# The feed-forward half of a decoder layer as one stage: gate, then up, then down, with the gate's extremes searched per tile

## The chip, the cores and the metric

One Trainium2 chip, one of its cores. The metric is the device time of one execution in microseconds (us). The kernel before takes 3091.08 us, the median of three runs (3089.62 to 3091.11).

## What is computed

A decoder layer on x of 16 x 512 rows of 512 numbers: gated linear attention, a decaying scan with a context, and a quantised feed-forward block, each followed by a residual and a layer norm. The change concerns the feed-forward block, which is

```python
def act_qdq(x):
    scale = max(max(abs(x)) / 32767, 1e-12)
    return clip(round(x / scale), -32768, 32767) * scale
x = act_qdq(x)
up = act_qdq(x @ lpbq_dequant(w_up).T)          # 512 -> 1536
gate = act_qdq(x @ lpbq_dequant(w_gate).T)      # 512 -> 1536
sig = fixed_qdq_u16(sigmoid(gate))              # steps of 2**-16
gate = act_qdq(gate * sig)
o = act_qdq(gate * up)
return o @ lpbq_dequant(w_down).T               # 1536 -> 512
```

The scale of each `act_qdq` is the largest magnitude of a whole tensor. So `gate` can't be rounded before all its products are known, nor `o` before its own largest value is.

## The kernel before, in words

`decoder` (L1630) runs five stages, each ending in a barrier of all engines: `prepare_weights`, `attention_phase`, `up_gate_phase` (L840), `scales_phase` (L1096) and `down_phase` (L1378). The first two are not changed. There are NB = 16 steps b of 512 rows. A step has 12 tiles of `up` and 12 of `gate`, each 128 outputs by 512 rows in one bank of PSUM; four tiles make a chunk of 128 x 2048 (48 chunks of each kind). Every engine has its program written out by hand, and the order within it is that of the code; semaphores join them.

**Up and gate.** `up_gate_phase` splits each operand into a high and a low float32r part (`qh`, `ql`, `wh`, `wl`), so a tile is 4 x 3 matmuls (L1062 to L1064). TensorE takes 24 tiles a step, groups of four of up and gate in turn. ScalarE evacuates each tile into a chunk `group` (L951) and takes the silu of gate chunks (L958). VectorE takes the largest magnitude of up chunks (L1001), the largest and the smallest product of gate chunks (L1004, L1005), and of silu times up (L1008, L1011), all in chunks of 2048 from SBUF. SyncE stores every chunk (L909). The next step's input is rounded on VectorE (L988), transposed by TensorE (L1054) in two halves after tiles 11 and 13, copied by ScalarE (L941), and its low part taken by VectorE (L993).

**Scales.** `scales_phase` reduces the maxima over the partitions (L1201, after one at the start of up and gate, L924), works the scales out in tiny VectorE instructions, decides (L1299) whether two chunks suffice to find the largest |o|, and loads these two chunks again (L1175, L1176), rounds and multiplies them whole, and reduces once more (L1209). TensorE has nothing to do meanwhile.

**Down.** `down_phase` loads every chunk of gate and up again as float32. GpSimd rounds both (L1485, L1490); ScalarE takes the sigmoid and rounds twice (L1515, L1519, L1524) and makes the high part (L1531); VectorE rounds the sigmoid (L1558), multiplies twice (L1560, L1566) and makes the low part (L1570), adds the residual (L1578) and takes statistics (L1581). TensorE does 48 matmuls a chunk (L1616 to L1618) into 8 banks, four for each of two steps. VectorE's order around a chunk is set by `chunk_steps` (L1425): a chunk is begun, the one before carried on, the one before that finished.

```python
                    pe.matmul(o, wh[:, m, k], qh[:, par, k], start=(k == 0), stop=False)
                    pe.matmul(o, wh[:, m, k], ql[:, par, k], start=False, stop=False)
                    mm = pe.matmul(o, wl[:, m, k], qh[:, par, k], start=False, stop=(k == KC - 1))
```

Of the kernel before, what the change touches and what calls it, by code (L numbers as in the profile page):

```python
# [837 lines left out]


def up_gate_phase(nc, x2_dram, w_ffn_t, up_dram, gate_dram, amax_x2, acc, rmax, scales):  # L840

    NM = 2 * MT
    GM = 4
    NG = NM // GM
    with ExitStack() as ctx:
        used = []
        ctx.callback(lambda: (nc.clear_and_free_semaphores(used), nc.all_engine_barrier()))  # L849

        def sb(name, shape, dt=F32):
            return ctx.enter_context(nc.sbuf_tensor(name, shape, dt))

        def sem(name):
            return phase_semaphore(nc, used, name)

        wh = sb("ug_wh", [P, NM, KC, P], F32R)
        wl = sb("ug_wl", [P, NM, KC, P], F32R)
        w_stage = sb("ug_w_stage", [P, 2, GM, KC * P])
        x2 = sb("ug_x2", [P, TT, HID])  # L860
        qh = sb("ug_qh", [P, 2, KC, T], F32R)
        ql = sb("ug_ql", [P, 2, KC, T], F32R)
        group = sb("ug_group", [P, 4, CH])
        silu = sb("ug_silu", [P, 2, CH])
        ident = sb("ug_ident", [P, P])
        step_max = sb("ug_step_max", [P, 3, 3])
        turn_ps = [ctx.enter_context(nc.psum_tensor(f"ug_turn{i}", [P, T], F32)) for i in range(2)]
        out_ps = [ctx.enter_context(nc.psum_tensor(f"ug_out{i}", [P, T], F32)) for i in range(6)]

        w_in = [sem(f"ug_w_in{i}") for i in range(2)]  # L870
        wh_ready, wl_ready = sem("ug_wh_ready"), sem("ug_wl_ready")
        x2_in = sem("ug_x2_in")
        stored = [sem(f"ug_stored{i}") for i in range(4)]
        consts, amax_all, scale_ready, inv_ready = sem("ug_consts"), sem("ug_amax_all"), sem("ug_scale_ready"), sem("ug_inv_ready")
        tq_ready, turned, qh_ready, ql_ready = sem("ug_tq_ready"), sem("ug_turned"), sem("ug_qh_ready"), sem("ug_ql_ready")
        out_ready, evacuated, silu_ready, prod_ready, rmax_ready = (
            sem("ug_out_ready"), sem("ug_evacuated"), sem("ug_silu_ready"), sem("ug_prod_ready"), sem("ug_rmax_ready"))
        step_max_ready, acc_ready = sem("ug_step_max_ready"), sem("ug_acc_ready")
        s_x, inv_x = scales[:, 0:1], scales[:, 1:2]

        def group_of(w, g):
            return w[:, g * GM:(g + 1) * GM].rearrange("p m k n -> p m (k n)")

        def slot(par, g):
            return (NG * par + g) % 4

        with nc.Block() as block:
            @block.sync
            def _(sp):
                sp.dma_start(x2[:], x2_dram[0]).then_inc(x2_in, 16)  # L890

                def load_weights(g):
                    if g < NG:
                        group_at = NWG // 3 * (g % 2) + g // 2
                        wait(sp, wl_ready, g - 1)
                        sp.dma_start(w_stage[:, g % 2], w_ffn_t[group_at]).then_inc(w_in[g % 2], 16)
                load_weights(0)
                load_weights(1)

                def step(b, par, nxt, first=False):  # L900
                    if nxt:
                        sp.wait_ge(turned, KC * (b + 1))
                        sp.dma_start(x2[:], x2_dram[b + 1]).then_inc(x2_in, 16)
# [193 lines left out]

# [584 lines left out]
```

## Time and profile before

| | us |
|---|---|
| median of three runs | 3091.08 |
| span of the profiled execution | 3087.7 |
| its own time (span and launch) | about 3.4 more than the span, taken from the median |
| attention and weights, until the first up/gate matmul | 1294.5 |
| up and gate, TensorE | 1294.5 to 2369.8 |
| TensorE idle (scales, start of down) | 2369.8 to 2460.6 |
| down, TensorE | 2460.6 to 3076.1 |
| busy: TensorE, VectorE, ScalarE, GpSimd | 2757.5, 2280.7, 1327.2, 588.0 |

Only the second half of the table can change, so it is to be read stage by stage: which engine is busy in it, and which wait holds TensorE.

### The profile page before, as it was taken

Reading aid. Unit: us, or ns where it says so; the run is one execution under the profiler, and the core shown is the slowest. Engines: PE = TensorE matmul, PEld = TensorE weight load, DVE = VectorE, ACT = ScalarE, POOL = GpSimd, SP = SyncE. Lnnn points to the kernel's source line nnn. Section 1 sums busy time; section 2 is a strip of 40 time slices with the busy share of each in tenths; the row PEclk is TensorE's granted clock in tenths of the full one; section 3 lists DMA queues with packets and bytes.
Section 4 is the critical chain, followed back from the end, with each engine's and each line's share of the span. In section 5 each row is a group of like instructions: output and inputs, shape, how many; then the busy total and the mean of one; then the engine's idle time right before and its main releaser. Section 6 shows DMA issues by size and latency. Waiting matters only on the chain. (4 is left out here: it accounts for less than half of the span.)

```text
span 3087.7 us, 32437 instructions
## 1 busy us (share of the span) xinstructions
PE 2757.5 (89%) x12272; PEld 2261.6 (73%) x12272; DVE 2280.7 (74%) x2242; ACT 1327.2 (43%) x1396; POOL 588.0 (19%) x266
## 2 busy tenths in 40 slices
PE   2589999999999999599999999999997198988988
PEld 2477777777777777488888888888885177777776
DVE  8678988889888998565555555555555688888886
ACT  2233433444333433243333333333333466666664
POOL 4111111112111111000000000000000485555552
PEclk7789999999999999899999999999998599999999
DMA  6211111111111111332222322222223555555552
GB/s 238 96 41 62 68 54 54 68 60 69 54 54 63 66 54 42 124 140 104 109 109 109 122 109 109 109 102 104 107 109 135 207 205 216 217 217 217 216 206 82
DMA packets 58129, 357.18 MB, mean 116 GB/s; under 512 B 6496, under 2 KB 6496, under 8 KB 17248
## 3 DMA queue, kind: packets, MB, share of 16 engines
q1 hardware_dynamic: 54480, 330.33, 28.5%
q10 hardware_dynamic: 3600, 26.22, 2.1%
q8 instruction: 29, 0.48, 0.1%
q14 instruction: 20, 0.16, 0.0%
HBM read 212.87 MB, written 143.65 MB: 115 GB/s over the span
## 5 line engine op out<-in xcount | busy, mean ns | idle before, releaser
L1062 PE MATMUL ug_out<-ug_qh,ug_wh 128*128 128x512 f32 x1536 | 601.3, 391 | 2.8 <-DVE ug_ql L993 1.4
L1064 PE MATMUL ug_out<-ug_qh,ug_wl 128*128 128x512 f32 x1536 | 598.5, 390 | 0.0
L1063 PE MATMUL ug_out<-ug_ql,ug_wh 128*128 128x512 f32 x1536 | 598.1, 389 | 0.0
L951 ACT ACTIVATE ug_group<-ug_out,scales 128x512 f32<-128x512 f32 x384 | 263.2, 690 | 607.3 <-PE ug_out L1064 604.5
L1616 PE MATMUL dn_ps<-down_wh,dn_oh 128*128 128x512 f32 x768 | 314.4, 409 | 148.3 <-DVE dn_ol L1570 148.3
L1004 DVE TENSOR_REDUCE ug_step_max<-ug_group 128x1 f32<-128x2048 f32 x48 | 109.7, 2285 | 335.4 <-ACT ug_group L951 335.4
L1062 PEld LDWEIGHTS ug_out<-ug_qh,ug_wh 128*128 128x128 f32 x1536 | 288.8, 188 | 62.6 <-DVE ug_wl L1016 2.0
L1064 PEld LDWEIGHTS ug_out<-ug_qh,ug_wl 128*128 128x128 f32 x1536 | 288.6, 188 | 60.5
L1063 PEld LDWEIGHTS ug_out<-ug_ql,ug_wh 128*128 128x128 f32 x1536 | 288.9, 188 | 59.0
L1617 PE MATMUL dn_ps<-down_wl,dn_oh 128*128 128x512 f32 x768 | 310.6, 404 | 0.0
L1618 PE MATMUL dn_ps<-down_wh,dn_ol 128*128 128x512 f32 x768 | 310.2, 404 | 0.0
L1616 PEld LDWEIGHTS dn_ps<-down_wh,dn_oh 128*128 128x128 f32 x768 | 151.8, 198 | 187.3 <-DVE dn_ol L1570 155.1
L717 PE MATMUL qk_ps<-xh,wah 128*128 128x512 f32 x512 | 201.4, 393 | 26.8 <-DVE xl L531 26.8
L1198 POOL MEMSET sc_magic<- 128x1 f32 x1 | 0.1, 99 | 1094.0 <-POOLq L849 1094.0
L718 PE MATMUL qk_ps<-xl,wah 128*128 128x512 f32 x512 | 200.7, 392 | 0.0
L721 PE MATMUL qk_ps<-xh,wal 128*128 128x512 f32 x512 | 200.6, 392 | 0.0
L449 ACT ACTIVATE phi<-qk_ps 128x1024 f32<-128x1024 f32 x64 | 65.9, 1029 | 263.6 <-PE qk_ps L721 263.6
L1001 DVE TENSOR_REDUCE ug_step_max<-ug_group 128x1 f32<-128x2048 f32 x48 | 109.7, 2286 | 90.3 <-ACT ug_group L951 90.3
L1617 PEld LDWEIGHTS dn_ps<-down_wl,dn_oh 128*128 128x128 f32 x768 | 152.3, 198 | 32.2
L1618 PEld LDWEIGHTS dn_ps<-down_wh,dn_ol 128*128 128x128 f32 x768 | 151.4, 197 | 33.0
L1485 POOL TENSOR_SCALAR dn_gate<-dn_gate,scales 128x2048 f32<-128x2048 f32 x48 | 168.6, 3512 | 0.0
L1515 ACT ACTIVATE dn_gs<-dn_gate,scales 128x2048 f32<-128x2048 int16 x48 | 96.6, 2013 | 152.3 <-POOL dn_gate L1485 152.3
(211 smaller groups left out, 5712.6 us busy)
## 6 DMA issues: line engine op xcount, KB each, us to landing
up_products<-ug_group SPq DMA_DIRECT2D x48, 1024.0 KB, 3.9
gate_products<-ug_group SPq DMA_DIRECT2D x48, 1024.0 KB, 3.9
dn_gate<-gate_products SPq DMA_DIRECT2D x48, 1024.0 KB, 4.9
dn_up<-up_products SPq DMA_DIRECT2D x48, 1024.0 KB, 4.8
xt_raw<-in_xT SPq DMA_DIRECT2D x64, 256.0 KB, 2.8
csq<-in_ctx_rows SPq DMA_DIRECT2D x16, 1024.0 KB, 6.7
xrow<-in_x_rows SPq DMA_DIRECT2D x16, 1024.0 KB, 4.8
x_rows<-xrow SPq DMA_DIRECT2D x16, 1024.0 KB, 3.9
```

Of the source, the lines that this page charges most:

```text
L717: pe.matmul(out, sh, mh, start=(k == 0), stop=False)
L718: pe.matmul(out, sh, ml, start=False, stop=False)
L721: mm = pe.matmul(out, sl_, mh, start=False, stop=(k == n - 1))
L951: act.activation(group[:, n % 4, m * T:(m + 1) * T], out_ps[(g * GM + m) % 6][:], ACT.Copy, scale=s_x).then_inc(evacuated, 1)
L1001: dve.tensor_reduce(step_max[:, 0, q:q + 1], part, AX.X, ALU.max, apply_absolute_value=True).then_inc(step_max_ready, 1)
L1062: pe.matmul(o, wh[:, m, k], qh[:, par, k], start=(k == 0), stop=False)
L1063: pe.matmul(o, wh[:, m, k], ql[:, par, k], start=False, stop=False)
L1064: mm = pe.matmul(o, wl[:, m, k], qh[:, par, k], start=False, stop=(k == KC - 1))
L1485: pool.tensor_scalar(gate[:, n], gate[:, n], inv_g, MAGIC, ALU.mult, ALU.add).then_inc(g_round, 1)
L1616: pe.matmul(o, oh[:, n, k, rows], mh, start=(n == 0 and k == 0), stop=False)
L1617: pe.matmul(o, oh[:, n, k, rows], ml, start=False, stop=False)
L1618: mm = pe.matmul(o, ol[:, n, k, rows], mh, start=False, stop=(n == NC3 - 1 and k == KC - 1))
```

## The change

The three stages become one, `ffn_phase`, with three passes over the 16 steps and no barrier between them. First all gate tiles (12 a step), then all up tiles, then down.

- **Gate pass.** TensorE transposes x2 as loaded, unrounded. ScalarE rounds while it evacuates (float32 in PSUM to int16 `q16`), then makes `hi` from it; VectorE makes `lo`. SyncE stores the rounded input to DRAM. After ScalarE has evacuated a tile, VectorE takes the largest and the smallest product from the PSUM bank itself, and the bank is free only after both.
- **Between gate and up.** The gate's scale and that of gate x sigmoid are worked out before the up pass.
- **Up pass.** The rounded input comes back from DRAM. Gate chunks are loaded, made int16 and sigmoid by ScalarE, the sigmoid is made uint16 by GpSimd, and one VectorE instruction gives the rounded product `gs16`, which is stored as int16. VectorE also takes the chunk's largest |up|, the product gs16 x up, and its maximum per 512 columns.
- **Scales.** Two pieces of 512 columns, instead of two chunks, are looked at again.
- **Down pass.** It loads up (float32) and gs16 (int16). GpSimd makes `up16`, VectorE the rounded product `o16` in one instruction, ScalarE `hi`, VectorE `lo`.
- **Weights.** There is room for 12 tiles, not 24: the up and down weights are loaded and split when the tiles of the last pass that use their place are done.

The core of the diff (the old phases go out whole, as told above):

```diff
+                def turn(b, par, tiles):                       # TensorE
+                    for c in tiles:
+                        wait(pe, q_ready, KC * b + c - 1)
+                        for j in range(TT):
+                            mm = pe.transpose(turn_ps[c % 2][:, j * P:(j + 1) * P],
+                                              x2[:, par, j * HID + c * P:j * HID + (c + 1) * P], ident[:])
+                def tile(s, par, m, first, gate):
+                        pe.wait_ge(evacuated, MT * s + m - 5)
+                            pe.wait_ge(gate_max_ready, 2 * (MT * s + m - 5))
+                def step(s, par, turn_next=False, weights=None, first=False, gate=True):
+                    pe.wait_ge(lo_ready, KC * (s + 1))
+                    for m in range(MT):
+                        if weights is not None and m % GM == 0:
+                            pe.wait_ge(wl_ready, weights + m // GM + 1)
+                        tile(s, par, m, first, gate)
+                        if m == 5 and turn_next:
+                            turn(s + 1, 1 - par, (0, 1))
+                        if m == 7 and turn_next:
+                            turn(s + 1, 1 - par, (2, 3))
...
+                def quantize(b, par):                          # ScalarE
+                    for c in range(KC):
+                        act.wait_ge(turned, KC * b + c + 1)
+                        act.activation(q16[:, par, c], turn_ps[c % 2][:], ACT.Copy, scale=inv_x).then_inc(q_ready, 1)
+                        act.wait_ge(q_ready, KC * b + c + 1)
+                        act.activation(hi[:, par, c], q16[:, par, c], ACT.Copy).then_inc(hi_ready, 1)
+                def gate_step(b, par, ahead, first=False):
+                    for g in range(NG):
+                        evacuate(b, par, g, range(GM))
+                        if first and g < NG - 1:
+                            weights_high(g + 1)
+                        if g == 1 and ahead:
+                            quantize(b + 1, 1 - par)
+                def up_step(b, par, ahead, first=False):
+                    for g in range(NG):
+                            act.wait_ge(up_max_ready, NG * (b - 1) + g + 1)
+                            act.wait_ge(prod_ready, NG * (b - 1) + g + 1)
+                        evacuate(NB + b, par, g, (0, 1))
+                            gate_chunk_16(nb, npar, ng, first and ng > 0)
+                        evacuate(NB + b, par, g, (2,))
+                            gate_chunk_sigmoid(nb, npar, ng)
+                        evacuate(NB + b, par, g, (3,))
+                        if first and g < NG - 1:
+                            weights_high(NG + g + 1)
+                        if not ahead:
+                            weights_high(2 * NG + g)
+                        if g == 1 and ahead:
+                            high(b + 1, 1 - par)
...
+                def gate_step(b, par, ahead, first=False):     # VectorE
+                    for g in range(NG):
+                        if g == 2 and ahead:
+                            low(b + 1, 1 - par)
+                        if first and g > 0:
+                            weights_low(g)
+                        for m in range(GM):
+                            dve.wait_ge(evacuated, n + 1)
+                            dve.tensor_reduce(gate_max[:, 0, bass.ds(n, 1)], ps, AX.X, ALU.max).then_inc(gate_max_ready, 1)
+                            dve.tensor_reduce(gate_max[:, 1, bass.ds(n, 1)], ps, AX.X, ALU.min, negate=True).then_inc(gate_max_ready, 1)
+                def up_step(b, par, ahead, first=False):
+                    for g in range(NG):
+                        if g == 2 and ahead:
+                            low(NB + b + 1, 1 - par)
+                        if first and g > 0:
+                            weights_low(NG + g)
+                        dve.wait_ge(evacuated, GM * (NG * (NB + b) + g + 1))
+                        dve.tensor_reduce(up_max[:, bass.ds(t, 1)], group[:, g], AX.X, ALU.max, ...)
+                        dve.tensor_tensor(prod[:, 0], gs16[:, g], group[:, g], ALU.mult).then_inc(prod_ready, 1)
+                        dve.wait_ge(prod_ready, t + 1)
+                        dve.tensor_reduce(cell_max[:, bass.ds(GM * t, GM)], prod[:, 0]..., AX.X, ALU.max, ...)
+                        if g < NG - 1 or ahead:
+                            gated(nb, npar, ng)     # scalar_tensor_tensor: gs16 <- sr16 (u16), g16 (i16)
+                def down_step(b, par, k=None, bias=True, ahead=True):
+                    product(b, par, 1)              # scalar_tensor_tensor: o16 <- gs16 (i16), up16 (i16)
+                    ol_chunk(b, par, 0)
+                        norm_bias(b - 2)
+                    product(b, par, 2)
+                    ol_chunk(b, par, 1)
+                        sums(b - 1, 1 - par, k)
+                        product(b + 1, 1 - par, 0)
+                    ol_chunk(b, par, 2)
...
+                def round_sigmoid(b, par, g, first=False):     # GpSimd, up pass
+                    pool.tensor_scalar(sr16[:, (NG * par + g) % 2], raw[:, g], 65536.0, 0.0, ALU.mult, ALU.add)
+                def round_up(b, par, g, first=False):          # GpSimd, down pass
+                    pool.tensor_scalar(up16[:, (NG * par + g) % 2], raw[:, g], inv_u, 0.0, ALU.mult, ALU.add)
...
+                def down_loads(b, par, k, ahead):              # SyncE
+                        sp.wait_ge(d_stored[par], 16 * k)
+                    sp.dma_start(x2_res[:, par], x2_dram[b]).then_inc(d_x2_in[par], 16)
+                        for g in range(NG):
+                            sp.wait_ge(up16_ready, t + 1)
+                            sp.dma_start(raw[:, g], up_dram[t + NG]).then_inc(d_up_in[g], 16)
+                            sp.wait_ge(o16_ready, t + 1)
+                            load_gs(b + 1, g)
```

## Rows read from the trace of the kernel before

**Rows 1.** Stages by --windows: busy time of each engine, then granted clock, DMA share, GB/s.

```profile
1380.00:2344.00 964.00, 964.00 (x4366) 800.47 (x4365) 535.40 (x299) 346.36 (x444) 0.00 (x0) 1.00 0.27 108
...
2470.00:3055.00 585.00, 527.39 (x2181) 429.10 (x2180) 511.59 (x389) 400.61 (x238) 336.03 (x147) 0.94 0.56 204
```

**Rows 2.** TensorE's timeline where stages meet: start, duration, then what it waited for.

```profile
1294.47 0.79 PE L1062 MATMUL ug_out<-ug_qh,ug_wh 128*128 128x512 f32 x1 [1.41 <-DVE ug_ql L993]
...
2369.45 0.39 PE L1064 MATMUL ug_out<-ug_qh,ug_wl 128*128 128x512 f32 x1
2460.56 0.80 PE L1616 MATMUL dn_ps<-down_wh,dn_oh 128*128 128x512 f32 x1 [90.72 <-DVE dn_ol L1570]
...
3075.71 0.39 PE L1618 MATMUL dn_ps<-down_wh,dn_ol 128*128 128x512 f32 x1
```

**Rows 3.** Waits between 2470 and 3055 us: total, times, longest.

```profile
POOL dn_tick L1484 <- DMA dn_up<-up_products: 222.8, 43, 11.3
...
PE dn_ps L1616 <- DVE dn_ol L1570: 57.6, 15, 6.0
```

**Rows 4.** Groups of instructions in up and gate, shapes apart: busy, mean ns, idle before.

```profile
L951 ACT ACTIVATE ug_group<-ug_out,scales 128x512 f32<-128x512 f32 x384 | 263.2, 690 | 607.3 <-PE ug_out L1064 604.5
...
L993 DVE TENSOR_TENSOR ug_ql<-ug_turn,ug_qh 128x512 fp32r<-128x512 int16 x64 | 41.2, 683 | 47.5 <-ACT ug_qh L941 47.5
L1054 PE MATMUL ug_turn<-ug_ident,ug_x 128*128 128x128 f32 x256 | 35.0, 282 | 24.4 <-DVE ug_x L988 23.6 <-DVE ug_ql L993 0.8
L941 ACT ACTIVATE ug_qh<-ug_turn 128x512 fp32r<-128x512 int16 x64 | 34.9, 596 | 80.1 <-PE ug_turn L1054 80.1
```

**Rows 5.** ScalarE's timeline around the transposes of one step: evacuations of tiles 11 and 14.

```profile
1730.62 0.69 ACT L951 ACTIVATE ug_group<-ug_out,scales 128x512 f32<-128x512 f32 x1 [2.03 <-PE ug_out L1064]
1733.35 0.69 ACT L951 ACTIVATE ug_group<-ug_out,scales 128x512 f32<-128x512 f32 x1 [2.04 <-PE ug_out L1064]
...
1743.32 0.69 ACT L951 ACTIVATE ug_group<-ug_out,scales 128x512 f32<-128x512 f32 x1 [0.96 <-PE ug_out L1064]
```

**Rows 6.** TensorE's timeline after a short and after a longer stall.

```profile
331.11 0.50 PE L717 MATMUL mix_ps<-ah,wah 128*128 128x512 f32 x1 [1.42 <-DVE att L612]
331.45 0.39 PE L718 MATMUL mix_ps<-al,wah 128*128 128x512 f32 x1
...
2718.73 0.80 PE L1616 MATMUL dn_ps<-down_wh,dn_oh 128*128 128x512 f32 x1 [4.37 <-DVE dn_ol L1570]
2719.32 0.63 PE L1617 MATMUL dn_ps<-down_wl,dn_oh 128*128 128x512 f32 x1
2719.75 0.63 PE L1618 MATMUL dn_ps<-down_wh,dn_ol 128*128 128x512 f32 x1
```

**Rows 7.** VectorE's timeline over one gate chunk in the loop of up and gate.

```profile
1703.63 2.28 DVE L1005 TENSOR_REDUCE ug_step_max<-ug_group 128x1 f32<-128x2048 f32 x1
1705.82 2.28 DVE L1008 TENSOR_TENSOR ug_silu<-ug_silu,ug_group 128x2048 f32<-128x2048 f32 x1
1708.23 2.29 DVE L1011 TENSOR_REDUCE rmax<-ug_silu 128x2048 f32 x1
```

**Rows 8.** Timelines of down, GpSimd and VectorE: alone, and beside each other.

```profile
2430.93 1.96 POOL L1485 TENSOR_SCALAR dn_gate<-dn_gate,scales 128x2048 f32<-128x2048 f32 x1
...
2477.65 6.13 POOL L1490 TENSOR_SCALAR dn_up<-dn_up,scales 128x2048 f32<-128x2048 f32 x1
...
2475.81 4.00 DVE L1566 TENSOR_TENSOR dn_up<-dn_gs,dn_up 128x2048 f32<-128x2048 int16 x1
```

**Rows 9.** Timelines by engine: a reduction, the decision, a load, its user.

```profile
1286.15 0.38 POOL L924 PARTITION_ALL_REDUCE amax_x<-amax_x  x1 [9.19 <-issue]
...
2384.66 0.15 DVE L1299 CAST sc_go_through<-sc_tmp 128x1 int32<-128x1 f32 x1
...
2387.46 0.36 SPq L1175 DMA_DIRECT2D sc_gate<-gate_products  x1
...
2394.56 2.09 ACT L1223 ACTIVATE sc_gate<-sc_gate,sc_magic,scales 128x2048 f32<-128x2048 f32 x1 [1.74 <-DMA sc_gate<-gate_products]
```

More of the change, by code:

```diff
@@ L1087, in quantizer @@
+GM = 4
+NG = MT // GM
+NS = 2 * NB
 def quantizer(dve, scale, inv, amax, sem, count):
@@ new lines, in high, with evacuate @@
+                def high(b, par):
+                    act.wait_ge(q_in[par], 16 * (b // 2 + 1) if isinstance(b, int) else 16 * ((b - par) >> 1) + 16)
+                    for c in range(KC):
+                        act.activation(hi[:, par, c], q16[:, par, c], ACT.Copy).then_inc(hi_ready, 1)
+                def evacuate(s, par, g, tiles):
+                    for m in tiles:
+                        n = MT * s + GM * g + m
+                        act.wait_ge(out_ready, n + 1)
+                        act.activation(group[:, g, m * T:(m + 1) * T], out_ps[(GM * g + m) % 6][:], ACT.Copy,
+                                       scale=s_x).then_inc(evacuated, 1)
@@ new lines, in _ @@
+                dve.wait_ge(gs_known, 1)
+                gated(0, 0, 0)
+                up_step(0, 0, True, True)
+                with dve.Fori(0, (NB - 2) // 2) as i:
+                    for u in range(2):
+                        up_step(2 * i + 1 + u, (1 + u) % 2, True)
+                up_step(NB - 1, 1, False)
+                dve.wait_ge(up_max_ready, NCH)
+                dve.tensor_reduce(packed[:, 0:1], up_max[:], AX.X, ALU.max).then_inc(packed_ready, 1)
+                dve.wait_ge(cell_ready, NCH)
@@ new lines, in _ @@
+                turn(0, 0, range(KC))
+                step(0, 0, True, 0, True)
+                step(1, 1, True)
+                with pe.Fori(1, (NB - 2) // 2) as i:
+                    for u in range(2):
+                        step(2 * i + u, u, True)
+                step(NB - 2, 0, True)
+                step(NB - 1, 1)
+                step(NB, 0, weights=NG)
+                step(NB + 1, 1, gate=False)
+                with pe.Fori(NB // 2 + 1, NB) as i:
+                    for u in range(2):
+                        step(2 * i + u, u, gate=False)
@@ L1610, in step, with down_step @@
+                def down_step(b, par):
+                    for g in range(NG):
+                        sl = (NG * par + g) % 2
+                        pe.wait_ge(ol_ready, NG * b + g + 1)
+                        if g == 0 and (not isinstance(b, int) or b > 1):
                             pe.wait_ge(sum_ready, TT * (b - 1))
```

1146 lines of the change are left out of this document (527 added, 619 removed).

## Prediction

> **What bounds the kernel now.** I read the stages first. In up and gate TensorE is busy all 964 us of the loop, at full granted clock (1.00), while VectorE, at 535 us, and ScalarE have room [rows 1]. The evacuations at 1730.62 and 1733.35 are one tile of 12 matmuls apart: 2.72 us, or 0.2266 a matmul [rows 5]. Nothing but fewer or better packed matmuls could shorten this stage. Then TensorE is idle for 90.7 us while the scales are found and down is filled [rows 2]. Down is another matter: its 48 chunks of 48 matmuls would take 16 x 144 x 0.2266 = 522 us, but TensorE's part runs from 2460.6 to 3075.9, 615.3 us, 38.5 us a step in place of 32.6. TensorE waits there for the low part of VectorE (57.6 us in 15 waits), and GpSimd for loads that are issued late (222.8 us in 43) [rows 3]. VectorE is busy 87% of that stage [rows 1]; it and GpSimd slow each other: a GpSimd rounding takes 1.96 us alone and 6.13 us beside VectorE's, a product of 2048 columns 4.00 us where one takes 2.28 alone [rows 7, 8]. So there are about 180 us to be had: 90 in the gap, 93 in down.
>
> The sum is made against the profiled execution (span 3087.7); the median of the runs, 3091.1, is 3.4 us more, which I add for launch. One per cent is 31 us; a measurement can tell about 0.2%, 6 us, from no change.
>
> **Start.** The barrier, the first reduction with its 9.19 us of issue [rows 9] and the first loads stay. TensorE may transpose without VectorE's rounding, but ScalarE has four more instructions. I take 1293.9 for the first matmul, against 1294.5 [rows 2].
>
> **Gate pass, a step.** 12 tiles take 32.6 us. Sixteen transposes take 1.8: evacuations of tiles 11 and 14 are 9.97 us apart, three tiles are 8.16 [rows 5]. Before, nobody waited, because two tiles of TensorE's work lay between the two halves and the copy came first. Now TensorE stands before the third group of four transposes right behind tile 7, until ScalarE has evacuated tile 7 and rounded the first group out of the same bank. Counted from the end of tile 7 (the modelled end, 0.16 after the next start): evacuation 0.04 to 0.73, rounding 0.62 to 1.31 (0.69 each [rows 4]), TensorE resumes at 1.37, a stall of 1.5. Then `hi` (0.60 [rows 4]) and the second rounding end at 2.5, while the transposes took 0.45: 0.8 more. Stall 2.3 us a step. VectorE has 24 searches of 512 columns, with that many columns and a source in PSUM as L993 at 0.68 [rows 4], so 16.4 us, and 2.7 for `low`: half of the step, hidden, and six banks give 13 us of room. Step: 36.8.
>
> The first step has weights on its path. At tile 4: evacuation of tile 3, high part of the next weights on ScalarE (about 2: a like instruction took 2.09 [rows 9]), low part on VectorE (2.28 for two tensors of 2048 [rows 7]), together 5.1 us of stall. At tile 8: evacuation, high weights, the whole rounding of the next step (5), `low`, low weights, 9.7 us besides the transposes. With the clock (below) three times 2.4: 56.4 us in all. The pass: 56.4 + 14 x 36.8 + 32.6 = 604, to 1898.
>
> **Clock.** After 1.42 us without work TensorE's next matmuls still last 0.39 us (2.4 GHz); this pair of rows occurs 14 times in attention. After 4.37 us they last 0.63, twelve of them, 0.43 apart (1.2 GHz) [rows 6]: 12 x 0.20 = 2.4 us. I charge 2.4 us to each stall over 3 us and nothing to those under 2; between 1.42 and 3 I have no row.
>
> **From gate to up.** Counted from the last gate tile's end. VectorE's last two searches end at 2.1, the reductions at 2.9, then come the low up weights and `low` of the first step, so TensorE restarts at 7.5. The partition reduction takes 0.38 [rows 9] and is hidden. But tile 4 needs `weights_low`, which VectorE does after the whole first up chunk, and that waits for a gate chunk: stores landed 4.7, load about 12 (a load asked at 2387.46 is used at 2394.56 [rows 9]), int16, sigmoid, and the fourth evacuation 22.7; then four VectorE operations of 2.3, then the weights: 34. TensorE was through with tiles 0 to 3 at 21. The second chunk does it again: from tile 7's evacuation, 9 for the chunk, 2.4 `low`, 2.2 weights. The up step 0 ends at 75 where 32.6 would be work: 42 us are lost here that the kernel before doesn't pay.
>
> **Up pass, a step.** Per chunk VectorE has a search, a product, a search and the int16 product. Spacing is 2.2 us, 2.4 where a wait and a loop's register stand between [rows 7]: 9.1 a chunk; three and `low` are 30 us against TensorE's 32.6, so VectorE is 92% full but no bound. The order is: `low` for the next step stands behind chunk 1, which can't begin before tile 7 is evacuated, 22.7 us into the step. 22.7 + 9.1 + 2.5 = 34.3 us: TensorE starts the next step 1.7 us late, every step. Of the int16 product I know no row; both sides: two tensors of 2048 columns take 2.28 us, spaced 2.2 [rows 7], which I take, since it is the nearest row; half of that is the other end. The Trainium skill, "VectorE: DVE Perf Modes", section What auto-detection actually checks, says that the engine doubles its pace if every tensor is 16-bit with step 1, as all three are here; the section on the tier table lists no scalar_tensor_tensor. By it the step would be 33.2 and the whole 15 us less; no row here shows it.
>
> GpSimd's rounding for the chunk after next begins when the sigmoid ends, at tile 7's end, and lasts 2.2, beside VectorE's search and before its product: no clash as I count, with 0.6 us to spare. A clash costs one 1.96 us rounding [rows 8], per step 28 us in all. The Trainium skill, "SBUF — State Buffer", section Who interferes with whom, says that a reduction never contends with GpSimd and an operation with two SBUF inputs does; the second half agrees with 4.00 against 2.28 [rows 7, 8], the first no row shows. DMA carries 8.4 MB a step, 245 GB/s; 204 take a share of 0.56 [rows 1], so 245 take about 0.67, no bound.
>
> The pass: 75 + 14 x 34.3 + 32.6 = 588, to 2486.
>
> **From up to down.** Counted from the last tile's end: chunk on VectorE to 7.6, packing and reduction 8.8, ten tiny instructions to the decision 10.8, the first load 2.65 later (as 2384.81 to 2387.46 [rows 9]) with three more, 15.4, landed 18.5, one copy of 1024 columns, a product, a search, 22.2, reduction, scales 25.4. GpSimd's first rounding is shut out by the low weights until 24.4, 26.5; then product, `hi` beside the second product, `low`: 35.7. I take 36, against 90.7 before. If GpSimd must load its reduction again, as L924's 9.19 us of issue before its first may mean [rows 9], it is 45. Down starts at 2522.
>
> **Down pass.** VectorE has per step three products, three `low` (2.2 each), and four sums and statistics of 512 columns (0.7 each, as L993 [rows 4], and 1 for the moments), 6.6: 20 us of 32.6. GpSimd has 3 roundings for 6. The loads shrink from 3 + 3 MB to 3 + 1.5. So TensorE bounds it: 522 + 2.4 for the clock, to 3046.3. The tail from the last matmul is unchanged: 3087.7 - 3075.9 = 11.8. Span 3058, time **3061 us**: 30 less. Gained 54 in the gap and 91 in down; lost 33 in transposes, 24 in up, 42 between the passes, 15 in the first step.
>
> **Rivals.** (a) *The clock falls at the short stalls.* The up pass's stall (1.7) and the gate's pair (1.5 and 0.8 with transposes of 128 columns between) lie just above the 1.42 that did no harm and well below the 3.84 us (57.6 / 15 [rows 3]) of the mean stall in down, after which it did fall. If both fell, 14 x 2.4 + 15 x 2.4 = 70 us: 3131, slower; one alone gives 3095, no change. It decides where a stall passes from 1.42 towards 3. (b) *Down keeps a loop of waits.* SyncE asks for the next up chunks only after the output store of the step before last: normalised 3.4 us before the step's start, stored at 4.5, loaded at 12, rounded at 16, product 18.3, `low` 20.6; TensorE needs it at 21.8. With contention as in rows 8 it misses by 2 us, and the clock adds 2.4: 14 x 4.4 = 60, 3121. For it: GpSimd waits for loads now too [rows 3]; against: 1.2 us are left. (c) *Better than counted:* int16 at double pace (-15) and transitions shorter by 10: 3036. (d) The decision goes the other way and all chunks are gone through: 48 chunks, some 15 us each, twice; over 1000 us more. The same decision takes the short way now.
>
> **Chances.** Forecast's case 0.54 (3046 to 3083); (c) 0.16; (a) with one stall 0.09, with both 0.07; (b) 0.08; rest, slower by contention or reloads, 0.05; (d) 0.01. Faster: 0.54, 0.16 and a little, 0.72; same, within 6 us, 0.09; slower 0.19. The range takes (c) and one of (a) whole: 3033 to 3118.
>
> **To look for.** TensorE's waits: a pair at the third and fourth transposes of each gate step, on `q16`, 2.3 us together; one of 1.7 at each up step, on `lo`; down without waits, 32.6 a step; gaps of 7.5, 13, 15 and 36 us. Matmuls of 0.63 us after the short stalls would prove (a), periods over 33 us in down (b), a gated product of 1.2 us (c).

## The result and the profile after

The changed kernel takes **3130.19 us**, the median of four runs (3128.29 to 3132.03); the kernel before takes 3091.1 in the same comparison. The ratio is 1.0126, with a 95% interval of 1.0112 to 1.0141: slower by 39 us (1.3%), where 3061 was forecast and 3033 to 3118 was the range. The span of the profiled execution is 3128.1 us, 70 more than the 3058 of the sum. Where the 70 us lie is seen stage by stage.

The windows of the changed kernel, one for each pass and one for the gap ahead of down (columns as in [rows 1]):

```profile
1292.00:1907.00 615.00, 573.47 (x2540) 468.84 (x2541) 290.52 (x445) 211.56 (x318) 0.00 (x0) 0.96 0.32 124
1908.00:2546.00 638.00, 556.28 (x2305) 452.14 (x2304) 501.30 (x274) 353.75 (x355) 109.35 (x97) 0.93 0.57 214
2546.00:2591.00 45.00, 0.00 (x0) 0.00 (x0) 23.50 (x27) 7.23 (x5) 11.71 (x9) 0.53 0.69 251
2591.00:3117.00 526.00, 524.80 (x2304) 434.04 (x2304) 320.54 (x312) 132.27 (x106) 192.55 (x106) 1.00 0.47 190
```

Down is now what was forecast: TensorE works through 525 of 526 us at a clock of 1.00, where it was busy 90% at 0.94 [rows 1]. The two passes ahead of it are the trouble. TensorE works 556 us of 638 in up, at a clock of 0.93; DMA, at a share of 0.57, isn't full. The waits of TensorE from 1292 us on (total, times, longest) name what holds it:

```profile
PE ff_ps L1578 <- DVE ff_lo L1335: 57.8, 16, 7.6
PE ff_ps L1618 <- DVE ff_lo L1510: 45.7, 1, 45.7
PE ff_ps L1578 <- DVE ff_wl L1329: 36.9, 4, 14.5
PE ff_ps L1567 <- ACT ff_q L1188: 30.9, 30, 3.2
```

The first line holds the 14 waits of 3.37 us at the up steps, the one of 7.61 between gate and up, and that of the very first step. The second is the gap ahead of down, against 90.72 [rows 2]. The third is the weights in the two first steps (4.90 and 5.39, then 12.08 and 14.49), and the last the pairs at the transposes of the gate steps. The forecast against it, from the starts of TensorE's matmuls:

| | forecast | measured |
|---|---|---|
| first gate matmul | 1293.9 | 1292.3 |
| gate pass, a step | 36.8 | 36.8 or 38.4 |
| end of the gate pass | 1898 | 1908 |
| gate to up, three waits | 7.5, 13, 15 | 7.6, 12.1, 14.5 |
| up pass, a step | 34.3 | 37.6 to 39.2, mostly 37.9, mean 38.0 |
| end of the up pass | 2486 | 2545.6 |
| up to down | 36 | 45.7 |
| down, first to last matmul | 524 | 524.8 |
| tail | 11.8 | 12 |

So the 70 us are three entries: 10 in the gate pass (12 behind its start, 1.6 early), 49.5 in the up pass (588 forecast, 637.5 measured), 9.7 in the gap.

**An up step.** The timeline of VectorE from chunk 1 to the end of `low`, in one step of the changed kernel:

```profile
2231.80 2.29 DVE L1369 TENSOR_REDUCE ff_up_max<-ff_group 128x2048 f32 x1 [1.57 <-ACT ff_group L1201]
2234.00 2.28 DVE L1372 TENSOR_TENSOR ff_prod<-ff_gs,ff_group 128x2048 f32<-128x2048 int16 x1
2236.41 2.29 DVE L1374 TENSOR_REDUCE ff_cell_max<-ff_prod 128x2048 f32 x1
2238.61 2.34 DVE L1358 SCALAR_TENSOR_TENSOR ff_gs<-ff_sr,ff_scales,ff_g 128x2048 int16<-128x2048 uint16 x1
2240.87 4.18 DVE L1335 TENSOR_TENSOR ff_lo<-ff_q,ff_hi 128x512 fp32r<-128x512 int16 x4
2244.98 2.27 DVE L1369 TENSOR_REDUCE ff_up_max<-ff_group 128x2048 f32 x1
```

GpSimd's timeline over the same stretch:

```profile
2231.08 1.90 POOL L1122 TENSOR_SCALAR ff_sr<-ff_raw 128x2048 uint16<-128x2048 f32 x1
2241.94 0.27 POOL L1121 TENSOR_TENSOR ff_tick<-ff_mhalf 128x1 f32<-128x1 f32 x1 [8.97 <-ACT ff_raw L1224]
2242.18 2.34 POOL L1122 TENSOR_SCALAR ff_sr<-ff_raw 128x2048 uint16<-128x2048 f32 x1
```

The chunk takes 9.07 us (2231.80 to 2240.87), the 9.1 of the forecast. Then the four instructions of `low` take 4.18 us in place of 2.5, and a rounding of GpSimd lies in them, itself slower (2.34) than the one at 2231.08 (1.90), which falls on a reduction. TensorE, whose last step had ended, starts when `low` does end (timeline of TensorE):

```profile
2245.19 0.79 PE L1578 MATMUL ff_ps<-ff_hi,ff_wh 128*128 128x512 f32 x1 [3.37 <-DVE ff_lo L1335]
2245.77 0.63 PE L1579 MATMUL ff_ps<-ff_lo,ff_wh 128*128 128x512 f32 x1
...
2247.91 0.45 PE L1578 MATMUL ff_ps<-ff_hi,ff_wh 128*128 128x512 f32 x1
2248.20 0.39 PE L1579 MATMUL ff_ps<-ff_lo,ff_wh 128*128 128x512 f32 x1
```

After the wait of 3.37 us its matmuls last 0.63 us (1.2 GHz), then 0.39 again (2.4 GHz). In all 14 steps the wait is 3.37 us and 6 to 14 such matmuls follow; in nine they begin right behind it, in five 0.6 to 1.3 us after the restart.

**A gate step.** TensorE's timeline at two pairs of waits, a step apart:

```profile
1411.21 0.66 PE L1567 MATMUL ff_ps<-ff_ident,ff_raw 128*128 128x128 f32 x4 [1.36 <-ACT ff_q L1188]
1412.45 0.66 PE L1567 MATMUL ff_ps<-ff_ident,ff_raw 128*128 128x128 f32 x4 [0.58 <-ACT ff_q L1188]
1412.86 0.47 PE L1578 MATMUL ff_ps<-ff_hi,ff_wh 128*128 128x512 f32 x1
1413.17 0.39 PE L1579 MATMUL ff_ps<-ff_lo,ff_wh 128*128 128x512 f32 x1
...
1448.04 0.66 PE L1567 MATMUL ff_ps<-ff_ident,ff_raw 128*128 128x128 f32 x4 [1.36 <-ACT ff_q L1188]
1449.28 1.12 PE L1567 MATMUL ff_ps<-ff_ident,ff_raw 128*128 128x128 f32 x4 [0.58 <-ACT ff_q L1188]
1450.04 0.78 PE L1578 MATMUL ff_ps<-ff_hi,ff_wh 128*128 128x512 f32 x1
1450.62 0.63 PE L1579 MATMUL ff_ps<-ff_lo,ff_wh 128*128 128x512 f32 x1
```

The pair was forecast as 1.5 and 0.8; it is 1.36 and 0.58 (1.45 and 0.52 in the first and the last of the 14). Behind the first pair shown the clock stays up, behind the second, equal to it, it is down. Of the 14 pairs of the later steps 7 do so, mostly every second one; such a step takes 38.4 us (1448.04 to the pair at 1486.46) in place of 36.8, 7 x 1.6 = 11 us in all.

**The gap ahead of down.** GpSimd's timeline:

```profile
2569.25 2.31 POOL L1160 PARTITION_ALL_REDUCE ff_amax_o<-ff_amax_o  x1 [11.09 <-DVE ff_amax_o L1487]
2580.35 0.18 POOL L1152 TENSOR_TENSOR ff_tick<-ff_mhalf 128x1 f32<-128x1 f32 x1 [8.79 <-issue]
2580.53 1.96 POOL L1153 TENSOR_SCALAR ff_g<-ff_raw,ff_scales 128x2048 int16<-128x2048 f32 x1
```

And VectorE's, from the last tiny instruction on the scales to the first products:

```profile
2572.36 0.16 DVE L1495 TENSOR_TENSOR ff_scales<-ff_tmp,ff_scales 128x1 f32<-128x1 f32 x1
2582.64 6.36 DVE L1504 SCALAR_TENSOR_TENSOR ff_sr<-ff_gs,ff_scales,ff_g 128x2048 int16<-128x2048 int16 x2 [10.11 <-POOL ff_g L1153]
```

The scales are known at 2572.52, 26.9 us after the last up tile (forecast 25.4). What follows the forecast set at nothing: GpSimd has reduced by 2571.56, its next instruction, a tiny one, starts 8.79 us later, and the profile shows no event that it waited for in that time. VectorE stands for its rounding 10.11 us.

The reduction between gate and up has such a stretch too:

```profile
1911.20 2.31 POOL L1113 PARTITION_ALL_REDUCE ff_gate_top_all<-ff_gate_top  x1 [626.02 <-DVE ff_gate_top L1397]
1924.92 0.18 POOL L1121 TENSOR_TENSOR ff_tick<-ff_mhalf 128x1 f32<-128x1 f32 x1 [11.40 <-issue]
```

Part of these 11.40 us is the wait for ScalarE's first sigmoid, which ends at 1921.77 (1919.76 and 2.01); some 3 us are left. They cost nothing here: VectorE has its first gated product at 1929.44 and then waits 0.37 us more for ScalarE's last tile of the up chunk.

### The profile page after: what moved, and what is told of

It reads as the page before. It is cut to its first block, busy times and chain, and to the rows that moved or that the text cites. A ratio compares the mean times of both kernels' runs of the same rounds, so it can differ in the third digit from the quotient of the medians.

```text
span 3128.1 us, 34255 instructions
## 1 busy us (share of the span) xinstructions
PE 2782.3 (89%) x12272; PEld 2273.7 (73%) x12272; DVE 2228.9 (71%) x2502; ACT 1191.4 (38%) x1420; POOL 532.3 (17%) x311
## 4 chain that ended last, share of the span: by engine, by line
PE 46%; DVE 7%; issue 3%; ACT 2%; POOL 0%; DVEq 0%; POOLq 0%; ACTq 0%
PE ff_ps L1578 10%; PE ff_ps L1579 10%; PE ff_ps L1580 10%; PE ff_ps L1618 5%; PE ff_ps L1619 5%; PE ff_ps L1620 5%; DVE ff_lo L1335 2%; DVE ff_up_max L1369 1%; DVE ff_prod L1372 1%; DVE ff_gs L1358 1%; PE ff_ps L1567 1%; ACT ff_q L1188 1%; DVE ff_wl L1329 0%; ACT ff_group L1201 0%; DVE ff_cell_max L1374 0%
## 5 line engine op out<-in xcount | busy, mean ns | idle before, releaser
L1578 PE MATMUL ff_ps<-ff_hi,ff_wh 128*128 128x512 f32 x1536 | 623.1, 406 | 94.7 <-DVE ff_lo L1335 57.8
L1579 PE MATMUL ff_ps<-ff_lo,ff_wh 128*128 128x512 f32 x1536 | 615.1, 400 | 0.0
L1580 PE MATMUL ff_ps<-ff_hi,ff_wl 128*128 128x512 f32 x1536 | 613.8, 400 | 0.0
L1201 ACT ACTIVATE ff_group<-ff_ps,ff_scales 128x512 f32<-128x512 f32 x384 | 264.8, 689 | 679.9 <-PE ff_ps L1580 667.0
L1578 PEld LDWEIGHTS ff_ps<-ff_hi,ff_wh 128*128 128x128 f32 x1536 | 300.2, 195 | 165.2 <-issue 53.0
L1580 PEld LDWEIGHTS ff_ps<-ff_hi,ff_wl 128*128 128x128 f32 x1536 | 298.7, 194 | 64.7
L1579 PEld LDWEIGHTS ff_ps<-ff_lo,ff_wh 128*128 128x128 f32 x1536 | 300.3, 196 | 62.0
L1618 PE MATMUL ff_ps<-ff_wh,ff_hi 128*128 128x512 f32 x768 | 299.9, 391 | 45.7 <-DVE ff_lo L1510 45.7
L1619 PE MATMUL ff_ps<-ff_wl,ff_hi 128*128 128x512 f32 x768 | 299.8, 390 | 0.0
L1620 PE MATMUL ff_ps<-ff_wh,ff_lo 128*128 128x512 f32 x768 | 299.6, 390 | 0.0
```

The source lines that it names most:

```text
L1201: act.activation(group[:, g, m * T:(m + 1) * T], out_ps[(GM * g + m) % 6][:], ACT.Copy, scale=s_x).then_inc(evacuated, 1)
L1578: pe.matmul(o, wh[:, m, k], hi[:, par, k], start=(k == 0), stop=False)
L1579: pe.matmul(o, wh[:, m, k], lo[:, par, k], start=False, stop=False)
L1580: mm = pe.matmul(o, wl[:, m, k], hi[:, par, k], start=False, stop=(k == KC - 1))
L1618: pe.matmul(o, hi[:, sl, k, rows], mh, start=(g == 0 and k == 0), stop=False)
L1619: pe.matmul(o, hi[:, sl, k, rows], ml, start=False, stop=False)
```

## The experiments

Each kernel is the changed one with the edit shown. Every ratio is to the kernel before, timed in the same rounds (its median lay between 3089.85 and 3091.76); a gain against the changed kernel is the difference from 1.0126, times 3091. Each ratio's interval is 0.0010 to 0.0017 to either side, so a gain is known to some 6 or 7 us, and where it is smaller, TensorE's waits tell more.

**1. The low part one chunk earlier.** The forecast's 1.7 us a step came from `low` behind chunk 1; here it stands behind chunk 0.

```diff
 def up_step(b, par, ahead, first=False):     # ScalarE
-    if g == 1 and ahead:
+    if g == 0 and ahead:
         high(b + 1, 1 - par)
...
 def up_step(b, par, ahead, first=False):     # VectorE
-    if g == 2 and ahead:
+    if g == 1 and ahead:
         low(NB + b + 1, 1 - par)
```

> Up pass alone: the high and low parts of the next step's input are made one chunk earlier (ScalarE after chunk 0's evacuations, VectorE before chunk 1), the rest is the changed kernel. My theory: the 3.37 us wait before each of 14 up steps comes only from the place of low behind chunk 1, and the slow matmuls from that wait. Then an up step takes 32.6 in place of 37.8 us, no slow matmuls in the up pass after its first step, and the time is 3130 - 14 x 5.2 = 3057 us. Rival: VectorE itself is the bound of the up pass (30 us of work, 32 with clashes, and waits of its own); then a step stays over 34 us and the time over 3077. Second rival: the clock falls from too little work in the pass, not from the wait; then slow matmuls stay and the step is about 34.4, 3082.

Measured: 3054.38 us, ratio 0.9881 (0.9864 to 0.9897), 76 us less than the changed kernel. One window of its up pass:

```profile
1980.00:2440.00 460.00, 460.00 (x2032) 381.09 (x2031) 434.52 (x225) 305.38 (x310) 114.31 (x86) 1.00 0.69 259
```

The row of `low` among its groups in the same window, and after it the only wait of TensorE from 1980 to 2545 us:

```profile
L1335 DVE TENSOR_TENSOR ff_lo<-ff_q,ff_hi 128x512 fp32r<-128x512 int16 x56 | 58.6, 1108 | 0.0
```

```profile
PE ff_ps L1618 <- DVE ff_lo L1510: 46.2, 1, 46.2
```

TensorE is never idle at the steps and its clock stays up, though VectorE is busy 94% and `low` is still slowed, to 1108 ns for one. The contention costs TensorE nothing once it doesn't wait for `low`. So a full VectorE was no bound; the place of `low` in its order was.

**2. The clash taken away, the order kept.** GpSimd waits for `low` before it rounds the next step's first chunk.

```diff
 elif ahead:                                  # GpSimd, up_step
+    pool.wait_ge(lo_ready, KC * (NB + b + 2))
     round_sigmoid(b + 1, 1 - par, 0)
```

> Up pass alone: GpSimd's rounding of the next step's first chunk waits until VectorE has made low; place and order of everything else stay. My theory: low takes 4.18 us in the changed kernel in place of 2.49 because that rounding holds the port, so here it takes 2.5 and the wait is 3.37 - 1.7 = 1.7 us in each of 14 steps; after a wait that short the clock stays up. Step 34.5 in place of 37.8, time 3130 - 14 x 3.3 = 3084 us. Rival: the clock falls after 1.7 us as well: step 36.1, 3106 us. Rival: low is slow for another reason: wait and time stay, 3130.

Measured: 3081.62 us, ratio 0.9971 (0.9959 to 0.9982), 48 us less than the changed kernel. Its waits of TensorE in the up pass:

```profile
PE ff_ps L1579 <- DVE ff_lo L1336: 23.5, 14, 1.7
```

And its row of `low` in the window of experiment 1:

```profile
L1336 DVE TENSOR_TENSOR ff_lo<-ff_q,ff_hi 128x512 fp32r<-128x512 int16 x52 | 32.4, 684 | 0.0
```

`low` is back at 684 ns, the wait is 1.68 us in all 14 steps, no matmul of these steps lasts 0.63 us, and a step takes 34.6 us. That is the up step of the forecast (34.3, a wait of 1.7). Of the 3.4 us a step that came back (38.0 less 34.6), 1.7 are the clash itself; the rest is the clock, which was down behind each wait of 3.37 us and behind none of 1.68.

**3. The third and fourth transposes one tile later.**

```diff
 def step(s, par, ...):                       # TensorE
-    if m == 7 and turn_next:
+    if m == (7 if first else 8) and turn_next:
         turn(s + 1, 1 - par, (2, 3))
```

> Gate pass alone: the second half of the transposes stands behind tile 8 in place of tile 7 (in the first step it stays). My theory: ScalarE has rounded both banks 2.5 us after the end of tile 7, a tile takes 2.72, so the pair of waits (1.36 and 0.58 us, with their restarts 2.26 lost) goes from 14 steps, and the clock, which fell after seven of them at 1.6 us each, stays up: gate step 34.4 in place of 36.8 and 38.4 in turn, time 3130 - 43 = 3087 us. Rival: the waits only move to the fourth group (each 0.5) and the clock still falls: 3110. Rival: the search in the accumulators becomes what holds TensorE, since low comes later: over 3115.

Measured: 3088.25 us, ratio 0.9992 (0.9983 to 1.0002), 41 us less. The window shows the gate pass without waits and the clock at 1.00, where the same window of the changed kernel has TensorE busy 436.56 us at 0.98:

```profile
1400.00:1860.00 460.00, 460.00 (x2131) 382.89 (x2130) 240.66 (x374) 176.88 (x269) 0.00 (x0) 1.00 0.34 135
```

A step of 36.8 us holds 32.6 for its tiles and 1.8 for its transposes, so the pair of waits and the restarts behind them cost 2.4; 14 x 2.4 are 34 and the clock's falls 11, 45 together, which the 41 measured bear out within their uncertainty. The waits of 3.37 us in up are as they were: the two passes are independent.

**4. Both roundings before the high parts.** To see which of the two short waits mattered for the clock, ScalarE here rounds both banks of a half before it makes either high part. The first wait stays, the second goes.

```diff
-    act.wait_ge(q_ready, KC * b + c + 1)
-    act.activation(hi[:, par, c], q16[:, par, c], ...)
+    if c % 2:
+        for d in (c - 1, c):
+            act.wait_ge(q_ready, KC * b + d + 1)
+            act.activation(hi[:, par, d], q16[:, par, d], ...)
```

> Gate pass alone: ScalarE rounds both transposed banks first and makes the two high parts after them, so that the fourth group of transposes no longer waits for a high part. My theory: the first wait stays at 1.36 us, the second falls from 0.58 to about 0, 0.6 us less a step, 9 in all. The open question is the clock, which fell after every second pair of waits, though waits of 1.68 us in the up pass never made it fall (14 of 14): if it is the sum of both waits (1.94) that counts, it stays up here and 7 x 1.6 = 11 us more are gained: 3110 us. If it falls by the transposes' place or for another reason, 3121 us.

Measured: 3110.64 us, ratio 1.0059 (1.0042 to 1.0076), 21 us less. Waits of TensorE from 1400 to 1860 us:

```profile
PE ff_ps L1569 <- ACT ff_q L1188: 17.7, 13, 1.4
```

The window of the same stretch:

```profile
1400.00:1860.00 460.00, 442.27 (x2037) 363.52 (x2036) 229.76 (x357) 161.86 (x256) 0.00 (x0) 1.00 0.33 129
```

A wait of 1.36 us (1.45 in the first and the last) is there in all 14 steps, and no matmul behind one is slow. The second wait was worth 14 x 0.58 = 8 us and, with the first just ahead of it, the clock's 11: 19 together. The edit also joins the third and fourth groups of transposes into one run; whether the clock went by the second wait or by the break between them the run can't tell apart.

**5. The gate searched in chunks.** The part of the change that its name stresses, undone: chunks of 2048 from SBUF, as in [rows 7], in place of tiles from PSUM.

```diff
-    for m in range(GM):
-        dve.wait_ge(evacuated, n + 1)
-        dve.tensor_reduce(gate_max[:, 0, bass.ds(n, 1)], ps, AX.X, ALU.max)...
-        dve.tensor_reduce(gate_max[:, 1, bass.ds(n, 1)], ps, AX.X, ALU.min, negate=True)...
+    dve.wait_ge(evacuated, GM * (t + 1))
+    dve.tensor_reduce(gate_max[:, 0, bass.ds(t, 1)], group[:, g], AX.X, ALU.max)...
+    dve.tensor_reduce(gate_max[:, 1, bass.ds(t, 1)], group[:, g], AX.X, ALU.min, negate=True)...
```

ScalarE now waits for the search before it writes the chunk again, and TensorE's banks are free after ScalarE's copy alone (not shown in the cut).

> Gate pass alone: VectorE searches the largest and smallest gate product in evacuated chunks of 2048 columns in SBUF, two instructions a chunk, in place of two a tile in the accumulators; TensorE's banks are free after ScalarE's copy alone. My theory: the search per tile was hidden (VectorE is half idle in the pass, 13 us of room in the banks), so its place is worth nothing inside the pass; only at its end the last search starts later and lasts 4.4 in place of 1.3 us, 3 us more before the first up step: 3130 + 3 = 3133 us. Rival: the accumulators' search holds banks and costs TensorE in every step; then the time falls by more than 10 us.

Measured: 3136.76 us, ratio 1.0146 (1.0129 to 1.0163). By the ratios alone that is no difference that can be told from the changed kernel's. The waits tell it: before the first up tile 10.44 us in place of 7.61, in the first gate step 7.49 in place of 4.90, and the waits of the later gate steps as before. The search tile by tile gains these 5.4 us at the two places where something stands behind it on VectorE, and no wait of TensorE shows a cost.

**6. The up weights earlier.** Their parts are made in the last gate step and, for the third group, before the first gated product, and loaded one transfer earlier.

```diff
 def up_step(...):                            # ScalarE; VectorE's weights_low(NG + g) likewise
-    if first and g < NG - 1:
-        weights_high(NG + g + 1)
...
 evacuate(NB - 1, 1, 1, range(GM))            # ScalarE, last gate step
 high(0, 0)
+weights_high(NG + 1)
 evacuate(NB - 1, 1, 2, range(GM))
+weights_high(NG + 2)
 def gate_step(...):                          # VectorE
+    if not ahead and g > 0:
+        weights_low(NG + g - 1)
...
-weights_low(NG)
+weights_low(NG + 2)                          # before gated(0, 0, 0)
```

> Between gate and up alone: the high and low parts of the up weights are made while the last gate step runs (first two groups) and while VectorE waits for the first gate chunk (the third), not behind the first up chunks. My theory: the waits of 12.1 and 14.5 us at tiles 4 and 8 of the first up step come from VectorE's order alone, and the 7.6 us before the step falls to 5.4; with two falls of the clock less, 31 to 33 us: 3098 us. Rival: the first chunks are late whatever the weights do, so TensorE stands at tile 6 for a bank until ScalarE has evacuated, some 10 us; then 3108.

Measured: 3103.34 us, ratio 1.0037 (1.0023 to 1.0051), 28 us less. The waits at tiles 4 and 8 of the first up step (12.08 and 14.49) are gone and the one before it is 5.41, not 7.61. Not all of it is kept: a wait of 3.51 us stands before step 1, where the changed kernel, late as it is there, has none.

**7. The roundings before the last reduction.** If GpSimd's 8.79 us are lost only on the way back from a reduction to ordinary work, it should help to round the first two up chunks ahead of the reduction.

```diff
+    round_up(0, 0, 0, True)                  # GpSimd, both branches of the decision
+    round_up(0, 0, 1, True)
...
 pool.wait_ge(o_max_part, 1)
 pool.partition_all_reduce(amax_o[:], amax_o[:], ...)
-round_up(0, 0, 0, True)
-round_up(0, 0, 1, True)
 round_up(0, 0, 2, True)
```

> Between up and down alone: GpSimd rounds the first two up chunks of the down pass before its last reduction over the partitions, not after it. In the changed kernel it issued nothing for 8.79 us after that reduction, and VectorE's first product waited 10.1 us for the rounding. My theory: those 8.8 us are a load of GpSimd's code when it goes from the reduction back to ordinary operations; here it falls beside the load of the two pieces, the first product starts when the scales are known, and the gap is 45.7 - 10 = 36 us, time 3120. Rival: the way back to the reduction costs a like load, which then stands on the path: gap unchanged or longer, time 3130 or more.

Measured: 3122.51 us, ratio 1.0102 (1.0085 to 1.0119), between the two expectations; the gap is 39.46 us against 45.72. GpSimd's timeline:

```profile
2564.57 0.18 POOL L1145 TENSOR_TENSOR ff_tick<-ff_mhalf 128x1 f32<-128x1 f32 x1 [7.52 <-issue]
...
2575.65 0.38 POOL L1165 PARTITION_ALL_REDUCE ff_amax_o<-ff_amax_o  x1 [5.88 <-issue]
2585.47 0.18 POOL L1145 TENSOR_TENSOR ff_tick<-ff_mhalf 128x1 f32<-128x1 f32 x1 [9.44 <-issue]
```

Time is lost both ways: 9.44 us behind the reduction, and now 5.88 ahead of it. In the changed kernel, where only a tiny fill (L1144) stood between this reduction and the one before, it started 0.11 us after its input was known (2569.14 and 2569.25); there it had waited 11.09 us for that input, which would hide such a stretch. The order alone doesn't get rid of the loss.

**8. ScalarE rounds the first two up chunks of down.** It is idle then. The counts that GpSimd waits for change with it and are left out here.

```diff
+def round_first():                           # ScalarE, both branches
+    for g in range(2):
+        act.wait_ge(d_up_in[g], 16)
+        act.activation(up16[:, g], raw[:, g], ACT.Copy, scale=inv_u).then_inc(up16_ready, 1)
...
-round_up(0, 0, 0, True)                      # GpSimd
-round_up(0, 0, 1, True)
+pool.wait_ge(up16_ready, 2)
```

> Between up and down alone: ScalarE, idle there, rounds the first two up chunks of the down pass; GpSimd starts with the third. Theory: GpSimd issues nothing for 9 us after each reduction and 6 before one that follows ordinary work, so neither stands on the path if nobody waits for GpSimd after its last reduction. First product at 2572.5 in place of 2582.6 and without the clash that held its second instruction, gap 45.7 to about 35; the third chunk's rounding comes 10 us after the reduction, in time for TensorE's third group. Time 3130 - 11 = 3119 us, below the 3122.5 of the kernel that rounds before the reduction. Rival: the third chunk is late and TensorE waits a few us there: 3122 or more.

Measured: 3119.22 us, ratio 1.0087 (1.007 to 1.0103), 12 us less; the gap is 34.12 us. VectorE's first product follows the scales at once, and GpSimd's stretch without an instruction is there, but beside other work. VectorE's timeline:

```profile
2572.57 4.62 DVE L1511 SCALAR_TENSOR_TENSOR ff_sr<-ff_gs,ff_scales,ff_g 128x2048 int16<-128x2048 int16 x2
2577.10 2.28 DVE L1517 TENSOR_TENSOR ff_lo<-ff_sr,ff_hi 128x2048 fp32r<-128x2048 int16 x1
```

GpSimd's:

```profile
2581.33 0.18 POOL L1152 TENSOR_TENSOR ff_tick<-ff_mhalf 128x1 f32<-128x1 f32 x1 [9.76 <-issue]
```

**9. The four together** (edits 1, 3, 6 and 8).

> The four remedies in one kernel: low and high one chunk earlier in the up pass, the transposes one tile later, the up weights earlier, the first two roundings of down on ScalarE. If the causes are separate, the gains add: 3130 - 76 - 42 - 27 - 11 = 2974 us. Rival: they overlap, since without the waits VectorE (94% busy in the up pass of the kernel with low earlier) or a bank becomes what TensorE waits for in the first up steps; then over 2985.

Measured: 2966.94 us, ratio 0.9599 (0.9583 to 0.9615). The single gains are 76, 41, 28 and 12 us, 157 together; it gained 163. They add up, within their uncertainty. From the first gate tile on, TensorE still waits 2.8, 5.4 and 34.2 us, and 4.9, 3.2 and 4.9 in the first gate step.

**10. And the first gate step.** The kernel of experiment 9, with the first gate step's weights made one group ahead too.

```diff
 quantize(0, 0)                               # ScalarE
+weights_high(1)
 def gate_step(...):
-    if first and g < NG - 1:
-        weights_high(g + 1)
+    if first and g == 0:
+        weights_high(2)
...
 low(0, 0)                                    # VectorE
+weights_low(1)
 def gate_step(...):
-    if first and g > 0:
-        weights_low(g)
+    if first and g == 1:
+        weights_low(2)
```

The third and fourth transposes come after tile 8 in the first step as well.

> As the kernel with all four, and in the first gate step the weights of the next group are made one group ahead, so that the waits of 4.9, 3.2 and 4.9 us in it go, with their falls of the clock: 13 to 16 us less than that kernel, 2960 us. Rival: the weights' load or low of step 0 comes later instead and half of it is lost: 2967.

Measured: **2947.23 us**, ratio 0.9538 (0.9522 to 0.9554), the best of all: 4.6% under the kernel before, 182 us under the changed one. The windows of its three passes:

```profile
1292.00:1840.00 548.00, 547.33 (x2523) 455.21 (x2524) 289.19 (x441) 212.23 (x318) 0.00 (x0) 0.99 0.36 139
1856.00:2374.00 518.00, 518.00 (x2287) 428.91 (x2286) 489.85 (x258) 347.18 (x351) 131.56 (x96) 1.00 0.68 256
2409.00:2940.00 531.00, 524.91 (x2304) 434.11 (x2304) 322.20 (x317) 134.65 (x110) 191.40 (x108) 0.99 0.47 190
```

All of TensorE's waits from 1292 to 2940 us:

```profile
PE ff_ps L1627 <- DVE ff_lo L1519: 34.2, 1, 34.2
PE ff_ps L1587 <- DVE ff_lo L1343: 8.2, 2, 5.4
```

TensorE is the bound in all three passes. What is left is the 34 us ahead of down, 5.4 ahead of up and 2.8 at the start.

## Why the prediction was wrong

The plan of the sum held; one clash and one price of the clock turned its sign. Point by point:

- **Start, gate to up, down, tail: right.** Down's 91 us were gained in full; the three waits between gate and up came within 1 us each, and the first gate step took some 56 us, as forecast. (Its loss stands as 15 us in the closing list of the forecast; the stalls and the clock of its own sum make 22. The 3061 doesn't rest on that entry.) Rival (b), a loop of waits in down, did not come: TensorE waits for nothing there. The decision (d) took the short way.
- **The up step: the step that failed.** The text counted the rounding that begins at tile 7's end and found "no clash". The rounding that mattered is the next one. It comes four tiles later (2231.08 and 2242.18, 11 us apart), so by the forecast's own figures it begins some 33.7 us into the step, within the `low` that was set from 31.8 to 34.3. The text had the price right in kind (1.96 us a clash) and put it aside as unlikely. The price of the clash in the sum was nothing; it and its consequence measured 3.4 us a step, and taken away in experiment 2 they left a step of 34.6.
- **A clash that lengthens a wait isn't priced by itself.** It was costed at 28 us for the pass; it cost some 48 (experiment 2), because the wait passed from 1.68, where the clock stays, to 3.37, where it falls in every step. Rival (a) named the mechanism and the place, and gave 3131 with both stalls; it had 0.07. It came by another road than it stated: not at 1.7 us, behind which the clock stayed up, but at 3.37. That its 3131 meets the 3130 measured is chance: its 70 us are two stalls of the clock, the 70 measured are 10, 49.5 and 9.7.
- **The clock in the gate pass.** "Nothing to those under 2" was wrong for a pair. Behind a wait of 1.36 alone the clock stayed up 14 times in 14 (experiment 4); where one of 0.58 followed four transposes later it was down 7 times in 14, and 6 in 14 in experiment 5. That is the pass's 11 us. The waits themselves were 0.4 shorter than forecast, but a step whose clock stayed up still took the 36.8.
- **The gap ahead of down: 9.7 us over.** The forecast named 45 for the case that GpSimd "must load its reduction again". It came to 45.7, and after the reduction, on the way back to ordinary work, not ahead of it. The term was taken at its lower end, though [rows 9] had shown 9.19 us ahead of the first reduction.
- **The gated product.** It takes 2.34 us for 2048 columns (L1358), all three tensors 16-bit with step 1, the pace of [rows 7], so rival (c) fell. The Trainium skill, "VectorE: DVE Perf Modes", section What auto-detection actually checks, gives the double pace only where the firmware has enabled the perf modes of the instruction, a condition that the prediction left out. This trace shows no double pace for scalar_tensor_tensor.
- **Reductions beside GpSimd.** A maximum takes 2.29 us at 2231.80 although GpSimd rounds from 2231.08 to 2232.98, and `low` goes from 684 to 1108 ns. The Trainium skill, "SBUF — State Buffer", section Who interferes with whom, has it so: a reduction doesn't contend with GpSimd, an instruction with two SBUF inputs does. These two rows agree with it.

Where the gain went, then: 136 us of the 145 forecast for the gap and down came in (45 and 91). The gate and up passes together take 1253 us (1292.3 to 2545.6), where 1075 was the work of the kernel before (1294.5 to 2369.8) and 1192 was forecast; the 61 between are the clash, the waits that it lengthened and the clock. Experiments 1, 3, 6 and 8 gained 157 us singly, and 163 together in experiment 9, by the order of the work and, in experiment 8, by the engine that does it; no instruction was made cheaper.

## What to carry to other kernels

Where an engine waits at each step for another's last item, lay out every instruction of the third engine over one whole period, those of the next step's data among them; and ask first whether the item can stand one place earlier, which here was worth 76 us and made the clash harmless. Price a short wait of TensorE with the clock: here a clash of 1.7 us, on top of a wait of 1.7, cost 3.4, and two short waits in a row were not two single ones. Where roundings follow a partition reduction on GpSimd and others wait for them, another engine can do the first of them, which here gained 12 us.

## What the runs showed of the hardware

- TensorE's clock, by the matmuls behind a wait (0.39 us at 2.4 GHz or 0.63 at 1.2): up after 1.36 us alone (14 of 14, experiment 4) and after 1.68 alone (14 of 14, experiment 2); down in half of the cases after 1.36, four transposes and 0.58 (7 of 14, changed kernel); down in every case after 3.37 (14 of 14), in five of them not at once.
- GpSimd starts nothing for 8.79 us (changed kernel), 9.44 (experiment 7) and 9.76 (experiment 8) after a partition reduction when the tiny product and the roundings follow, and for 5.88 us ahead of a reduction that follows them (experiment 7). Not every instruction pays it: behind the first reduction, of x, the one that fills `ident` starts at once (1284.83, by the row below). The Trainium skill, "GPSIMD Engine Reference", section Instruction dispatch, gives some 6 us for the first call of freshly loaded code; that code is loaded again at each of these changes is not shown, only that the time is lost each time.

```profile
1284.56 0.38 POOL L1108 PARTITION_ALL_REDUCE amax_x<-amax_x  x1 [9.65 <-issue]
1284.83 0.35 POOL L1110 TENSOR_SCALAR_AFFINE_SELECT ff_ident<-ff_ident 128x128 f32<-128x128 f32 x1
```

- The reduction of the largest product (one column) took 2.31 us in the changed kernel and 0.38 in experiment 7, behind the 5.88 without issue. Why is open.
